# Rest rows of the down products packed with zeros, and a unit's weight parts in four wide pieces

## The reference

```
xn   = layernorm(x)
Wg, Wu, Wd = NF4[codes] * scales        # I x H, I x H, H x I; H = 1024, I = 2752
gate, up = xn @ Wg.T, xn @ Wu.T
f    = (silu(gate) * up) @ Wd.T
out  = x + s * silu(f)                  # s = xn + attention message
```

## Time and profile before

| what | value |
|---|---|
| median of three runs | 2484.89 us |
| the profiled execution, its own time | 2484.12 us |
| its span, first to last instruction | 2482.3 us |
| busy: TensorE, VectorE, ScalarE, GpSimd | 97%, 65%, 41%, 3% |
| mean granted TensorE clock | 0.989 of full |
| HBM traffic | 577.5 MB, 233 GB/s |

### The profile page before, as it was taken

One profiled execution on the slowest core, in us unless ns is written; L12 is line 12 of the kernel. 1 busy time (PEld: TensorE's weight loads), 2 busy tenths in 40 slices (PEclk: granted clock), 3 DMA queues, 4 the chain that ended last, 5 costly groups with the idle time before them and its releaser, 6 DMA issues.

```text
span 2482.3 us, 30225 instructions
## 1 busy us (share of the span) xinstructions
PE 2407.4 (97%) x11214; PEld 1107.6 (45%) x11214; DVE 1605.8 (65%) x2757; ACT 1006.0 (41%) x1145; POOL 83.4 (3%) x72
## 2 busy tenths in 40 slices
PE   2899999999999999999999999999999999999999
PEld 2444444444444444444444444444444444444444
DVE  8888787668998867788888886565422422421431
ACT  8877777777878443544445421110010000001001
POOL 0000000000000000000000000000010011001001
PEclk7899999999999999999999999999999999999999
DMA  6855776657766895566655544248867767777764
GB/s 244 258 173 181 246 250 205 199 178 255 247 237 213 282 360 194 174 218 216 217 193 197 200 146 142 94 181 316 322 259 315 298 245 290 301 284 287 299 258 165
DMA packets 172127, 579.52 MB, mean 233 GB/s; under 512 B 17648, under 2 KB 42912, under 8 KB 154188
## 3 DMA queue, kind: packets, MB, share of 16 engines
q1 hardware_dynamic: 136716, 289.21, 34.4%
q10 hardware_dynamic: 35264, 288.37, 29.9%
HBM read 388.76 MB, written 188.75 MB: 233 GB/s over the span
## 4 chain that ended last, share of the span: by engine, by line
PE 88%; DVE 4%; ACT 3%; issue 3%; DMA 2%; POOL 0%; SPq 0%; ACTq 0%; POOLq 0%; DVEq 0%
PE ps L1813 56%; PE ps L1958 31%; ACT arena L792 1%; DMA arena<-in_x 1%; PE ps L1886 1%; ACT arena L805 1%; PE ps L1767 1%; DVE arena L1334 0%; DVE arena L1265 0%; DVE arena L1423 0%; DVE arena L1308 0%; DMA arena<-in_gu 0%; ACT arena L957 0%; DVE arena L1355 0%; POOL arena L761 0%
## 5 line engine op out<-in xcount | busy, mean ns | idle before, releaser
L1813 PE MATMUL ps<-arena 128*128 128x512 f16 x7152 | 1554.0, 380 | 12.4 <-ACT arena L995 6.8
L1813 PEld LDWEIGHTS ps<-arena 128*128 128x128 f16 x7152 | 700.1, 98 | 853.6 <-ACT arena L995 7.3
L1958 PE MATMUL ps<-arena 128*128 128x512 f16 x3696 | 797.9, 379 | 0.0
L792 ACT ACTIVATE arena<-arena,bias_t 128x2048 f32<-128x2048 f32 (+3 forms) x288 | 525.0, 1830 | 79.8 <-DMA arena<-in_dn 68.7
L1958 PEld LDWEIGHTS ps<-arena 128*128 128x128 f16 x3696 | 361.6, 98 | 436.1
L1423 DVE TENSOR_TENSOR arena<-arena 128x512 f16<-128x512 f32 x364 | 243.2, 684 | 11.7 <-ACT arena L957 10.4
L1221 ACT ACTIVATE arena<-arena,e_d 128x512 f32<-128x512 f32 x48 | 34.6, 721 | 424.3 <-DVE arena L1732 219.4
L1005 ACT ACTIVATE arena<-ps,gate_back 128x512 f32<-128x512 f32 x84 | 57.1, 680 | 305.6 <-PE ps L1813 305.5
L761 POOL TENSOR_TENSOR arena<-arena 128x512 f32<-128x512 f32 x64 | 81.5, 1280 | 2384.6 <-DMA arena<-in_xt 2076.2
L1708 DVE SCALAR_TENSOR_TENSOR arena<-arena,sc 128x512 f32<-128x512 f32 x192 | 129.8, 744 | 0.0
L1015 ACT ACTIVATE arena<-arena,gate_back 128x512 f32<-128x512 f32 x84 | 60.4, 720 | 161.5 <-DVE arena L1596 152.1
(11 more groups left out here) (108 smaller groups left out, 1167.4 us busy)
## 6 DMA issues: line engine op xcount, KB each, us to landing
isc<-arena SPq DMA_DIRECT2D x308, 256.0 KB, 2.6
arena<-wdsc ACTq DMA_DIRECT2D x28, 2816.0 KB, 10.2
arena<-isc ACTq DMA_DIRECT2D x28, 2816.0 KB, 18.1
arena<-xnsc SPq DMA_DIRECT2D x48, 1024.0 KB, 8.6
wsc<-arena ACTq DMA_DIRECT2D x21, 1792.0 KB, 6.7
arena<-in_x SPq DMA_DIRECT2D x48, 512.0 KB, 5.6
arena<-in_gu ACTq DMA_DIRECT2D x43, 512.0 KB, 4.6
wdsc<-arena SPq DMA_DIRECT2D x77, 256.0 KB, 2.1
```

The lines of the kernel that those rows point to most:

```text
L792: a_.activation(buf, src, ACT.Prelu, bias=bias_t[:, i:i + 1], scale=scale, alpha=alpha).then_inc(ramps, 1)
L1813: ins = t_.matmul(ps[:, bank, :], wreg[:, b, w, wa, k, :], xreg[:, j, o, k, xa, :], start=start and (k, wa, xa) == (0, 0, 0), stop=stop an ...
L1958: ins = t_.matmul(ps[:, bank, :], ring_w[b][:, k, wa, g, :], ring_i[b][:, k, xa, :], start=first and (k, wa, xa) == (0, 0, 0), stop=r not ...
```

## The change

Part 1. For operands 1, 2 and 3 (PACKED) the rest block is stored in another form. The input side, isc, gets in block 10 its 64 real rows' high part in rows 0 to 63 and their low part in rows 64 to 127, one block in place of two. The weight side, wdsc, gets as first block high above high, and as second block low above zeros, the zeros copied from rows of a low part that are zero (ZEROS). The product then takes two matmuls for this block, both with the same moving block. SP has more waits and stores, ScalarE's ring loads wait for them (pack_out) and read 21 of 22 kB a row for these operands.

Part 2. The seven operands of a unit's weights are cast and subtracted in four groups, (4, 5), (0, 1), (2, 6), (3,), three of them 1024 columns wide. The places in the steps are set anew for both engines, and in step 3 the ramps are divided otherwise. Two of the four subtractions of early_sums become one.

The diff, cut to its core (waits whose counts change from seven to four a unit, and semaphores, are left out):

```diff
 X_ORDER = [0, 4, 1, 2, 5, 6, 3]
-W_ORDER = [0, 4, 5, 6, 1, 3, 2]
+W_ORDER = [(4, 5), (0, 1), (2, 6), (3,)]
 D_ORDER = [0, 4, 5, 1, 3, 6, 2]
...
 W_AT[2] = [(2, i) for i in range(4)]
-W_AT[3] = [(2, i) for i in (4, 5, 6, 7, 9, 8, 10, 11, 12)] + [(3, i) for i in range(4)]
+W_AT[3] = [(2, i) for i in (4, 5, 6, 7, 8, 9)] + [(3, i) for i in range(4)]
 for _s in range(4, 40):
...
     if _j == 0:
-        W_AT[_s] = [(_u + 1, i) for i in (4, 5, 6, 7, 9)]
+        W_AT[_s] = [(_u + 1, i) for i in (4, 6, 7, 5)]
     else:
-        W_AT[_s] = [(_u + 1, i) for i in (8, 10, 11, 12)] + [(_u + 2, i) for i in range(4) if _u + 2 < LAST or i == 0]
-W_AT[40] = [(LAST, 6)]
+        W_AT[_s] = [(_u + 1, i) for i in (8, 9)] + [(_u + 2, i) for i in range(4) if _u + 2 < LAST or i == 0]
+W_AT[40] = [(LAST, 4)]
 STORE_W_AT = {0: 1, 3: 2, 40: LAST}
...
+PACKED = (1, 2, 3)
+ZEROS = {1: (1, 2), 2: (), 3: (3,)}
 STAGED = {}
...
 SOON_CUT = [0, 8, 13, 18, 18, 18, 18]
-W_CUT = {5: [0, 0, 0, 1, 2, 3, 5], 8: [0, 0, 0, 1, 2, 3, 8], 13: [0, 0, 3, 5, 6, 6, 13], 4: [0, 0, 0, 0, 0, 0, 4],
-         9: [0, 0, 0, 0, 0, 0, 9], 1: [0, 0, 0, 1, 1, 1, 1], 0: [0] * 7}
-W_CUT[9], W_CUT[5], W_CUT[6] = [0, 0, 2, 3, 4, 5, 9], [0, 0, 0, 1, 3, 4, 5], [0, 0, 0, 1, 3, 4, 6]
-W_CUT[8] = [0, 0, 0, 2, 3, 4, 8]
+W_CUT = {10: [0, 0, 1, 4, 4, 4, 10], 6: [0, 0, 0, 1, 2, 2, 6], 4: [0, 0, 0, 1, 2, 3, 4], 3: [0, 0, 0, 1, 2, 2, 3],
+         2: [0, 0, 0, 1, 2, 2, 2], 1: [0, 0, 0, 1, 1, 1, 1], 0: [0] * 7}
...
         sa, sb_ = carve(172, 2), carve(174, 2)
+        sums = carve(172, 4)
         blk = carve(176, 8).rearrange("p (r a t) -> p r a t", r=2, a=2)
...
-        def w_source(u, o):
+        def w_source(u, ops):
             tg, tu = yb[2 * (u % 2)], yb[2 * (u % 2) + 1]
-            return {0: tg[:, 0:512], 1: tg[:, 512:1024], 3: tu[:, 512:1024], 4: sa, 5: sb_, 2: sa, 6: sb_}[o]
+            if ops == (3,):
+                return tu[:, 512:1024].rearrange("p (o c) -> p o c", o=1)
+            return (tg if ops == (0, 1) else sums).rearrange("p (o c) -> p o c", o=2)
+        def w_dest(u, ops, part):
+            return wflat[:, wbuf(0, u), ops[0]:ops[-1] + 1:max(1, ops[-1] - ops[0]), part, :]
...
                 n = STAGED[c + (o,)]
+                src = stage[SLOT[n]]
+                last = NDOWN - 1
                 if c[0] == "d":
...
                     dst = wdsc[o, :, c[1], :, :]
+                    if c[1] == last and o in PACKED:
+                        sp.dma_start(wdsc[o, 0:RR, last, :, :], src[RR:P]).then_inc(pack_out[o], 16)
+                        for to in ZEROS[o]:
+                            sp.dma_start(wdsc[to, RR:P, last, 1, :], src[0:RR, 1, :]).then_inc(pack_out[o], 16)
+                        src, dst = src[RR:P, 0, :], wdsc[o, RR:P, last, 0, :]
                 else:
...
                     dst = isc[c[2], o, :, c[1], :, :] if c[0] == "i" else xsc[c[1] - 2, o, :, c[2], :, :]
-                sp.dma_start(dst, stage[SLOT[n]]).then_inc(st_out[SLOT[n]], 16)
+                    if c[0] == "i" and c[1] == last and o in PACKED:
+                        src, dst = src[RR:P], isc[c[2], o, :, last, 0, :].rearrange("(s p) t -> p s t", s=2)
+                sp.dma_start(dst, src).then_inc(st_out[SLOT[n]], 16)
...
                     sp.wait_ge(prod, len(PRODS))
+                    if n == 1:
+                        for k in (4, 5):
+                            sp.wait_ge(st_out[k], 16 * SLOT.count(k))
                 sp.dma_start(xn_r[n % 2], xnsc[tp // 2, kt, :, :, :]).then_inc(xn_in[n % 2], 16)
...
-            def w_high(u, o):
-                b = wbuf(0, u)
-                it = w_base(u, 6, 1)
-                act.wait_ge(w_it, it + {0: 1, 1: 1, 3: 2, 4: 3, 5: 4, 2: 5, 6: 6}[o])
+            def w_high(u, n):
+                ops = W_ORDER[n]
+                act.wait_ge(w_it, w_base(u, 6, 1) + [4, 1, 6, 2][n])
                 if u >= 2:
                     act.wait_ge(wst[u % 2], 16 * (u // 2))
-                    act.wait_ge(prod, prod_at(step_of(0, u - 2, 1), {n: p for p, n in OPERAND.items()}[o]))
-                if o == 0 and u == 1:
+                    for o in ops:
+                        act.wait_ge(prod, prod_at(step_of(0, u - 2, 1), {k: p for p, k in OPERAND.items()}[o]))
+                if n == 0 and u == 1:
                     act.wait_ge(sc_out, 9 * 16)
-                src = w_source(u, o)
-                a_.activation(wflat[:, b, o, 0, :], src, ACT.Copy).then_inc(w_hi, 1)
+                a_.activation(w_dest(u, ops, 0), w_source(u, ops), ACT.Copy).then_inc(w_hi, 1)
...
                             act.wait_ge(st_out[k], 16 * slot_uses(k, last))
+                if i < 7 and o in PACKED:
+                    for k in PACKED:
+                        if k == o or o in ZEROS[k]:
+                            act.wait_ge(pack_out[k], 16 + 16 * len(ZEROS[k]))
                 act.dma_start(ring_wf[b], wdsc[o, :, :, :, :].rearrange("p k s c -> p (k s c)")).then_inc(rw_in[b], 16)
-                act.dma_start(ring_if[b], isc[tp, o, :, :, :, :].rearrange("p k s c -> p (k s c)")).then_inc(ri_in[b], 16)
+                n = (2 * NDOWN - (1 if o in PACKED else 0)) * CH
+                act.dma_start(ring_if[b][:, 0:n], isc[tp, o, :, :, :, :].rearrange("p k s c -> p (k s c)")[:, 0:n]).then_inc(ri_in[b], 16)
...
             early_high(1, 1)
-            for o in (0, 4, 5):
-                w_high(0, o)
+            for n in (0, 1):
+                w_high(0, n)
             ramp(1, 8)
...
             early_high(2, 1)
-            for o in (6, 1, 3, 2):
-                w_high(0, o)
+            for n in (2, 3):
+                w_high(0, n)
             for n in range(9, 12):
...
             p1_copy(0)
-            w_high(1, 0)
             for n in range(13, 16):
...
             sil_a(0)
-            for o in (4, 5, 6, 1, 3, 2):
-                w_high(1, o)
+            for n in range(4):
+                w_high(1, n)
             early_highs(4, 2, 0, 2)
...
                 if s == 3:
-                    for o in (0, 4, 5):
-                        w_high(2, o)
+                    w_high(2, 0)
...
                 if not late:
-                    ramps_of(s, 0, 2)
+                    ramps_of(s, 0, 1 if s == 3 else 2)
                 if half_tile_at(s, "p6"):
...
                 if 4 <= s < 40 and u + 1 != LAST:
-                    for o in ([0, 4, 5], [6, 1, 3, 2])[j]:
-                        w_high(u + 1, o)
+                    for n in ([0], [2, 3])[j]:
+                        w_high(u + 1, n)
                 if s == 4:
...
                     sil_a(s - 1)
                 if s == 3:
-                    w_high(2, 6)
+                    w_high(2, 1)
+                elif 4 <= s < 40 and u + 1 != LAST and not j:
+                    w_high(u + 1, 1)
                 if s < TOTAL:
...
                 if s == 3:
-                    for o in (1, 3, 2):
-                        w_high(2, o)
-                ramps_of(s, 0 if s == 4 else 3 if late else 2, 4)
+                    for n in (2, 3):
+                        w_high(2, n)
+                ramps_of(s, 0 if s == 4 else 3 if late else 1 if s == 3 else 2, 4)
                 if job:
...
                     else:
-                        dve.wait_ge(w_lo, 7 * LAST)
+                        dve.wait_ge(w_lo, 4 * LAST)
                 elif w or n >= 2:
-                    dve.wait_ge(w_lo, 7 * w + [0, -1, 2, 3][n])
+                    dve.wait_ge(w_lo, 4 * w + [0, 0, 1, 1][n])
                 if n == 0:
...
                     w_sum(u, i - 2, parts)
-                elif i == 7 or i == 9:
-                    w_sum(u, 2 if i == 7 else 3, parts)
-                else:
-                    n = {4: 0, 5: 1, 6: 2, 8: 3, 10: 4, 11: 5, 12: 6}[i]
-                    o = W_ORDER[n]
-                    dve.wait_ge(w_hi, w_base(u, 7, 1) + n + 1)
-                    v_.tensor_tensor(wflat[:, b, o, 1, :], w_source(u, o), wflat[:, b, o, 0, :], ALU.subtract).then_inc(w_lo, 1)
+                elif i == 6 or i == 7:
+                    w_sum(u, i - 4, parts)
+                else:
+                    n = {4: 0, 5: 1, 8: 2, 9: 3}[i]
+                    ops = W_ORDER[n]
+                    dve.wait_ge(w_hi, w_base(u, 4, 1) + n + 1)
+                    v_.tensor_tensor(w_dest(u, ops, 1), w_source(u, ops), w_dest(u, ops, 0), ALU.subtract).then_inc(w_lo, 1)
...
                     dve.wait_ge(e_lo, NG * e)
-                v_.tensor_tensor(early_t[:, 1, :], b[:, 0, 1, :], b[:, 0, 0, :], ALU.subtract).then_inc(ep_made, 1)
-                v_.tensor_tensor(early_t[:, 3, :], b[:, 1, 1, :], b[:, 0, 1, :], ALU.subtract).then_inc(ep_made, 1)
-                dve.wait_ge(ep_made, 4 * e + 1)
+                v_.tensor_tensor(early_t[:, 1:4:2, :], b[:, :, 1, :], b[:, 0, :, :], ALU.subtract).then_inc(ep_made, 1)
+                dve.wait_ge(ep_made, 3 * e + 1)
                 v_.tensor_tensor(early_t[:, 2, :], b[:, 1, 1, :], early_t[:, 1, :], ALU.subtract).then_inc(ep_made, 1)
```

(29 more changed lines are left out.)

9 lines of the change are left out of this document (4 added, 5 removed).

## The result

The changed kernel took 2478.81 us in the median of 13 runs (2477.38 to 2480.3), the kernel before 2484.55 beside it. The ratio is 0.9979, 95% interval 0.9971 to 0.9987. The forecast was 2474.7 with a range from 2471.5 to 2478.5; the time lies just outside it. Timed again later, in another group of kernels, the changed kernel gave 0.9979 again (0.997 to 0.9988).

What follows compares the result with a forecast made beforehand. TensorE bounds the kernel, busy 2407.4 of 2482.3 us, with few, early waits. 2484.12 - 10.35 (packing) + 1.3 + 1.0 - 2.1 = 2474.0; with the median 0.8 above that execution, 2474.7 us, range 2471.5 to 2478.5.

Steps and rivals of the forecast that it cites:

- (b): Second unit: VectorE waits for the wide cast, TensorE goes on at about 113.8 instead of 112.58; +1.3 us, bounds -0.5 and +2.5.
- (c): Step 3: ramps end at 166.0, VectorE waits 1.5 us for them; +1.0 us at 194.51, bounds 0 and +2.
- (d): Later odd steps: 0.6 us less ScalarE work shortens four small waits, 260 to 430 us; 2.1 gained, bounds 0 and 3.5.
- (a): First unit: wide lows and merged subtractions make the first product about +0.6 us late, bounds 0 and +1; not added.
- inside this gap: Claim that the first unit's +0.6 us is contained in TensorE's later start after the copy of p1.
- falls into ScalarE's idle time: Even steps: wide cast of operands 0 and 1 behind the sigmoid unit fits 5.76 us idle before 292.61; costs nothing.
- Rival A: Colder start after longer waits: half clock may cost 1.7 us at 194.51; then 2476.4, or up to 2478; chance 0.18.
- Rival D: Wide cast of operands 0 and 1 makes VectorE late in 18 even steps, 17.3 us, so 2492; chance 0.03.

## Why the prediction was wrong, step by step

The sum put the stages ahead of the down stage at +0.2 us: +1.3 for (b), +1.0 for (c), -2.1 for (d). They measured +4.62. Ahead of the wait in step 9, where (b) and (c) have done their work and (d) begins, TensorE was 3.20 late (263.38 for 260.18), against 2.3 forecast. From there to the down stage it lost another 1.42, against 2.1 to be gained. So of the 4.4 us by which this sum was off, 3.5 are (d)'s and 0.9 are (b)'s and (c)'s.

- **Part 1** was right to the digit: 48 matmuls, 10.35 us forecast and 10.36 seen, no wait in the down stage, no cost at the hand-over (-11.0 when done alone).
- **Part 2, prices** were nearly right: 1.218 and 1.047 us for the wide instructions, 1.218 and 1.057 forecast. The durations of a narrow and a wide cast, 0.616 and 1.047, leave a fixed part of 0.185 us. The Trainium skill ("VectorE: DVE Perf Modes", section on the TRN2 errata) gives 224 cycles, 0.187 us, and the trace agrees. The prediction's "no row here has two casts that far apart" was wrong: the earlier trace rows has 0.619 and 1.057, which leave 0.18. What a merge frees is less, since neighbours overlap by 0.1.
- **(a)** looks right, 0.55 for 0.6, and that is luck: executions of one kernel differ by as much at this point (75.41 and 75.92 for the changed one).
- **(b)** looks right, 1.15 for 1.2 at the copy of p1, and is half luck. The 0.55 of the start is in it, which the prediction held to be "inside this gap". Counted from the execution's first product, TensorE went on behind the copy of p1 after 37.20 to 37.23 us in all five profiled kernels with narrow pieces and after 37.81 to 37.83 in all eight with wide ones: 0.60 later, half of the forecast. VectorE's wait for the wide cast was as forecast (1.12 for 1.2); but its multiply ahead of it (L1338) began 14.40 us after the first product and not 14.92, since the ramps that it waits for came earlier, which the prediction had only in its lower bound. "The chain through early blocks 6 and 7 shifts alike" was wrong: block 6's load was issued 1.10 late and landed at 116.12 for 115.80, only 0.3 late.
- **(c)** named a wait that is there and a path that is not, and missed the one that is. I followed the ramps, found VectorE's wait for them rightly (1.5 forecast, 1.70 seen at 166.87) and carried it to step 6 as +1.0. With the ramps left in place and the piece early, step 6 began 119.24 us after the first product, and 119.14 before the change: the codes' landing hides it. What I did not ask is who wants each piece first, and where it now stands. Operand 6's low part is wanted by p7 of the very next step, and with operand 2 it moved from slot 3 to slot 5. Putting it back took the wait from 5.43 to 2.43. p7 was 4.81 late, of which 1.6 came back by step 9, as step 6's own wait of 1.66 was covered. So the sum of (b) and (c) came out inside their bounds, by another path.
- **(d) is the step that failed most, in its sign**: -2.1 forecast with bounds from -3.5 to 0, +1.42 measured. Odd steps did have 0.6 us less of casts, and one wait, that before p1 of step 17, fell from 1.26 to 0.66 by exactly this. But the cast that moved into the even step delays the job's last casts, these VectorE's gating of the odd step, and this ScalarE's list there; "falls into ScalarE's idle time" was read from a step with 5.76 us of it, and behind the sigmoid unit of step 16 there is none. The wait near 265 stayed (2.11 and 2.08), that near 420 grew to 2.08 from 1.22, by 0.94 of the cast, 0.54 of the wide low part and -0.62 of the shorter casts. With the cast at the end of the step it was 1.41. And the clock drop behind it cost 1.7.
- **Rival A** was right in kind and wrong in place: a clock drop after a longer wait cost 1.7 us, but at 424, not at 195, where there was no wait left.
- **Rival D** named the mechanism of (d), and its even steps, but priced it as a loss in each of 18 steps. It bites where ScalarE has no slack, once with a visible price.
- **The range's** upper edge, 2478.5, was drawn 0.5 below what the bounds of the terms give, 2479, without a reason; the measured 2478.81 lies between the two. The bounds themselves had (d) at 0 at worst and no price for a piece that comes too late for its first user, the one thing that a new order can always cost.

Not settled: how the 5.7 us of part 2 are divided between waits and clock from execution to execution, since a profile shows one of them; and why the clock falls after some waits and not after others.

## What to carry to other kernels

When small pieces are merged or reordered, list for each piece its first user and both its old and its new place; the price is there, not in the instructions saved. An engine's idle time is to be read in the step in question, not in a better one. When two executions are laid side by side, count from a common point such as the first product, or the scatter of the start passes for an effect. Before moving an instruction earlier on account of a wait for a load, look whether the DMA engines are full: here only the load that went ahead of the batch gained.

## What the runs showed of the hardware

A wait of the same length can be followed by half the clock (1.2 GHz) or not. After the wait for the evacuation in step 9 the clock held in the kernel before (2.11 us), in both profiles of the changed kernel (2.08, 2.09) and with the wide pieces alone (2.08); it dropped with the piece early (2.08) and in three packed kernels with narrow pieces (2.12 to 2.13). In packing alone it held even after 3.11 us before 160.64. The Trainium skill ("TensorE: Matmul & The Clock Gate", part 1) has the clock fall after idleness and return under work. Each drop in these rows agrees, as it stands behind a wait and ends while TensorE works; which wait brings one, no row here shows. A drop cost 1.7 us after the shorter waits (32.94 for 31.25 us of 144 matmuls, 61.43 for 59.77 of 276) and 2.0 after 5.43 us (92.77 for 90.82 of 420), as much as many of the waits themselves. So removed waits were worth anything from nothing (2.4 us less before 157.80, and 2474.4 for 2472.6) to half as much again as their length (the 0.73 and 2.65 us gone, and 2469.27 for 2474.4).

When a load lands depended on what else was in flight. With the DMA engines at a share of 1.0, codes asked for 2.0 us earlier (168.65 for 170.62) were there 0.7 later; asked for at 161.82, ahead of the batch, they were there when ScalarE wanted them at 166.82.
